# A decoder in one program: explicit orders at both ends of slot attention, other positions in both context attentions and the last feed-forward

## The reference, cut to what matters

```python
x = x + L0_attn(_layernorm(x))              # gated slot attention, 16 heads of 128, 64 slots
x = x + L0_xattn(_layernorm(x), ctx_2048)   # 256 queries on 1344 text and 257 image keys, two softmaxes
x = x + L0_ffn(_layernorm(x))               # 8 experts, top 2, and a base expert
x = x + L1_attn(_layernorm(x))              # differential attention
x = x + L1_xattn(_layernorm(x), ctx_2048)   # 256 queries on the 1601 context rows, causal at the end
x = x + L1_ffn(_layernorm(x))               # 704 inner columns, silu(g) * u
```

## Time and profile before

| | us |
|---|---|
| median of three runs | 1824.39 |
| lowest, highest run | 1814.95, 1839.33 |
| the profiled execution | 1826.9 |
| its span, first to last instruction | 1825.0 |
| mean granted TensorE clock | 0.972 |

### The profile page before, as it was taken

One profiled execution on the slowest core, in us unless ns is written; L12 is line 12 of the kernel. 1 busy time (PEld: TensorE's weight loads), 2 busy tenths in 40 slices (PEclk: granted clock), 3 DMA queues, 4 the chain that ended last, 5 costly groups with the idle time before them and its releaser, 6 DMA issues.

```text
span 1825.0 us, 51399 instructions
## 1 busy us (share of the span) xinstructions
PE 1649.1 (90%) x21686; PEld 1161.5 (64%) x21686; DVE 1279.3 (70%) x2850; ACT 855.8 (47%) x1404; POOL 558.6 (31%) x951
## 2 busy tenths in 40 slices
PE   5999999999867899899899889998988898899988
PEld 4899999998653455465466545664554455566557
DVE  6778777877577787877888353444367687888844
ACT  3343434433350465656666712442343466567652
POOL 5553544534142130501502031441021222431230
PEclk9999999999988999999999989998999999999999
DMA  3000100110008364262362383653812245554100
GB/s 127 23 25 1 47 13 13 53 43 1 20 10 172 56 132 98 47 152 51 84 119 49 70 322 111 226 185 101 160 24 40 46 82 133 87 106 77 24 2 24
DMA packets 91857, 143.94 MB, mean 79 GB/s; under 512 B 14870, under 2 KB 60123, under 8 KB 91628
## 3 DMA queue, kind: packets, MB, share of 16 engines
q1 hardware_dynamic: 87228, 127.79, 30.1%
q10 hardware_dynamic: 2528, 7.74, 1.3%
q0 software_dynamic: 1872, 5.13, 0.7%
HBM read 109.68 MB, written 32.03 MB: 78 GB/s over the span
## 4 chain that ended last, share of the span: by engine, by line
PE 67%; DVE 18%; ACT 5%; issue 5%; POOL 2%; DMA 1%; SPq 1%; DVEq 0%; ACTq 0%; POOLq 0%
PE bank L1076 17%; PE bank L1284 6%; PE bank L2029 6%; DVE shared L1357 4%; PE bank L1915 4%; PE bank L1917 3%; PE bank L1916 3%; PE bank L808 3%; PE bank L2048 3%; DVE xa_part_max L1357 3%; PE bank L2476 2%; ACT xa_e L1318 2%; PE bank L773 2%; PE bank L747 1%; PE bank L2491 1%
## 5 line engine op out<-in xcount | busy, mean ns | idle before, releaser
L1357 DVE TENSOR_REDUCE xa_part_max<-bank 128x1 f32<-128x448 f32 (+1 forms) x512 | 266.0, 567 | 22.3 <-PE bank L1076 20.3
L1318 ACT ACTIVATE xa_e<-bank 128x1024 f32<-128x1024 f32 (+1 forms) x208 | 212.2, 1024 | 124.6 <-PE bank L1076 122.5
L1318 ACT ACTIVATE ca_e<-bank 128x1024 f32<-128x1024 f32 (+2 forms) x208 | 197.4, 958 | 78.0 <-PE bank L1076 75.6
L1357 DVE TENSOR_REDUCE shared<-bank 128x1 f32<-128x400 f32 (+1 forms) x384 | 205.0, 569 | 29.2 <-PE bank L1076 25.8
L1076 PE MATMUL bank<-xa_kst,xa_qst 122*32 122x448 bf16 (+1 forms) x2048 | 182.5, 351 | 17.3 <-DVE xa_part_max L1357 9.7
L1284 PE MATMUL bank<-xa_e,xa_vaug 128*17 128x256 f32 (+1 forms) x1664 | 134.3, 381 | 6.8 <-ACT xa_e L1318 4.3
L1076 PE MATMUL bank<-xa_qst,xa_kst 128*32 128x256 bf16 (+1 forms) x3264 | 135.2, 274 | 1.3 <-DMA xa_qst<-xa_negT 1.3
L1284 PE MATMUL bank<-ca_e,ca_vaug 128*17 128x256 f32 (+2 forms) x1664 | 125.4, 373 | 3.6 <-ACT ca_e L1318 2.5
L1012 POOL TENSOR_TENSOR gsa_qk<-gsa_qk,gsa_rot 128x512 f32<-128x512 f32 x64 | 81.8, 1279 | 142.3 <-DVE gsa_rot L928 142.3
L1076 PE MATMUL bank<-xa_wkv,shared 128*32 128x256 f32 (+1 forms) x1632 | 112.6, 386 | 11.2 <-issue 4.4
L1076 PEld LDWEIGHTS bank<-xa_qst,xa_kst 128*32 128x32 bf16 (+1 forms) x3264 | 93.1, 97 | 31.8 <-issue 3.4
(11 more groups left out here) (408 smaller groups left out, 4181.0 us busy)
## 6 DMA issues: line engine op xcount, KB each, us to landing
xa_kst<-xa_k_parts SPq DMA_DIRECT2D x96, 200.1 KB, 5.0
ca_kst<-ca_k_parts SPq DMA_DIRECT2D x96, 200.1 KB, 5.2
xa_k_parts<-xa_parts SPq DMA_DIRECT2D x24, 400.2 KB, 4.7
ca_k_parts<-moe_ctx_parts SPq DMA_DIRECT2D x8, 1200.8 KB
moe_gu<-in_expert_gate_up SPq DMA_DIRECT2D x8, 1024.0 KB
shared<-in_ctxT_split ACTq DMA_DIRECT2D x4, 1601.0 KB, 8.7
moe_ctxT<-in_ctxT SPq DMA_DIRECT2D x8, 800.5 KB, 8.1
ca_cv<-in_ctx SPq DMA_DIRECT2D x4, 1536.0 KB
```

The source lines that it names most:

```text
L1318: e.activation(self.e[m % 3][0:rows, :, first:T], banks[m % 2][0:rows].rearrange("p a (h t) -> p (a h) t", t=T)[:, :, first:T], ACT.Exp, s ...
L1357: e.tensor_reduce(top, work[:, 0:hi - lo], AX.X, ALU.max).then_inc(*reduced(t, *step))
```

## The change

No instruction is added or removed; the lists are put in another order.

In slot attention `first_turns` writes out turns 0 to 3 with the norms in between, and `last_turns` turns 15 to 18 with the preparation of cross attention; turns 4 to 14 stay. In cross attention, keys, turns, queries, values and stores of the later batches get other positions, and the maxima of a unit other stretches, by its place in the batch. In context attention `pv`, `acc`, `fin`, `neg_parts`, `neg_turn`, the norms, hidden sums (`hid`), values, weights, loads and maxima move, and so do the steps of the feed-forward. The diff, cut:

```diff
+            def first_turns():
+
+                yield from (
+                    ("norm_stats", 0, 0, 2), ("norm_turn", 0, 0), ("norm", 0, 0), ("norm_turn", 0, 1), ("h_split", 0), ("w_split", 0, "q"), ("norm", 0, 1),
+                    ("w_split", 0, "k"), ("norm_stats", 0, 2, 8), ("u", 0), ("norm", 0, 2), ("qk", 0), ("norm", 0, 3), ("norm", 0, 4), ("qk", 1), ("norm_turn", 0, 2),
+                    ("norm_turn", 0, 3), ("h_split", 1), ("qk", 2), ("a", 0), ("u", 1), ("norm", 0, 5), ("norm_turn", 0, 4), ("es", 0), ("w_split", 0, "v"), ("a", 1),
+                    ("qk", 3), ("w_split", 0, "g"), ("qk", 4), ("norm_turn", 0, 5), ("ok", 0), ("h_split", 2), ("a", 2), ("norm", 0, 6), ("qk", 5), ("ok", 1), ("u", 2),
+                    ("cs", 0), ("a", 3), ("norm_turn", 0, 6), ("v", 0, 0), ("qk", 6), ("ok", 2), ("es", 1), ("a", 4), ("norm", 0, 7), ("et", 0), ("sm_max", 0),
...
+                    ("qk", 14), ("qk", 15), ("a", 12), ("v", 2, 1), ("w2", 3, 1), ("wo", 0, 0), ("wo", 0, 1), ("sm_max", 2), ("a", 13), ("o", 3))
...
-                if m == GSA_UNITS:
-                    yield "xa_w", 2
-                    for n in range(XA_TILES):
-                        yield "xk", 0, n
-                    yield "k_norm", 0
-                if m == GSA_UNITS + 1:
-                    q_steps, k_steps = list(queries(0)), list(xa_keys(0))
-                    yield from q_steps[:TB + 1]
-                    yield from k_steps[:8]
-                    yield from q_steps[TB + 1:]
-                    yield from k_steps[8:]
-                    yield "load", 0
...
-            yield from norm_steps(0, 0)
-            yield "h_split", 0
-            yield "w_split", 0, "q"
-            yield "w_split", 0, "k"
-            yield "norm_stats", 0, TB, NT
-            yield from normed_rows(1)
-            yield from normed_rows(2)
-            yield from normed_rows(3)
-            for m in range(GSA_UNITS + 3):
-                if m < GSA_UNITS - 1:
-                    main = list(turn(m))
-                else:
-                    main = list(weave(list(weave(list(scores(m)), list(ahead(m)))), list(behind(m)), lead=8))
-                if m < GSA_UNITS + 2:
-                    yield from weave(main, list(xa_early(m)))
-                else:
-                    yield main[0]
-                    yield from (("xv", 0, n) for n in range(XV_EARLY))
-                    yield from main[1:]
+
+            def last_turns():
+
+                yield from (
+                    ("qk", 60), ("sm_exp", 13), ("ok", 56), ("v", 14, 0), ("a", 58), ("scale", 12, 0), ("es", 15), ("rr", 12), ("ok", 57), ("a", 59), ("xa_w", 2),
+                    ("qk", 61), ("z", 26), ("gate", 26), ("z", 27), ("cs", 15), ("gate", 27), ("ot", 12, 0), ("sm_max", 14), ("scale", 12, 1), ("w2", 26, 0), ("ok", 58),
+                    ("w2", 26, 1), ("ok", 59), ("a", 60), ("ot", 12, 1), ("qk", 62), ("sm_exp", 14), ("wo", 12, 0), ("wo", 12, 1), ("ok", 60), ("w2", 27, 0),
+                    ("norm_stats", 1, 0, 2), ("w2", 27, 1), ("a", 61), ("o", 26), ("a", 62), ("norm", 1, 0), ("v", 14, 1), ("o", 27), ("ok", 61), ("qk", 63), ("z", 28),
...
+                    ("z", 29), ("w2", 28, 1), ("norm_turn", 1, 0), ("a", 63), ("xk", 0, 3), ("xk", 0, 4), ("xk", 0, 5), ("xk", 0, 6), ("ot", 13, 0), ("xk", 0, 7),
+                    ("norm", 1, 1), ("xk", 0, 8), ("xk", 0, 9), ("o", 28), ("ok", 63), ("wo", 13, 0), ("v", 15, 0), ("xk", 0, 10), ("sm_max", 15), ("w2", 29, 0),
+                    ("w2", 29, 1), ("norm_turn", 1, 1), ("xk", 0, 11), ("xk", 0, 12), ("gate", 29), ("q", 0), ("k_norm", 0), ("sm_exp", 15), ("o", 29), ("ot", 13, 1),
+                    ("q", 1), ("rr", 14), ("q_norm", 0), ("k_scale", 0, 0), ("k_scale", 0, 1), ("q_store", 0), ("k_scale", 0, 2), ("gate", 30), ("scale", 14, 0),
+                    ("scale", 14, 1), ("k_scale", 0, 3), ("k_scale", 0, 4), ("k_turn", 0, 0), ("k_scale", 0, 5), ("wo", 13, 1), ("k_store", 0, 1, None), ("ot", 14, 0),
+                    ("k_scale", 0, 6), ("z", 30), ("w2", 30, 0), ("k_turn", 0, 1), ("k_scale", 0, 7), ("norm_stats", 1, 2, 4), ("norm", 1, 2), ("k_turn", 0, 2),
+                    ("z", 31), ("k_scale", 0, 8), ("v", 15, 1), ("w2", 30, 1), ("k_turn", 0, 3), ("xv", 0, 0), ("norm_turn", 1, 2), ("q_turn", 0), ("k_turn", 0, 4),
+                    ("k_turn", 0, 5), ("ot", 14, 1), ("k_turn", 0, 6), ("o", 30), ("w2", 31, 0), ("k_scale", 0, 9), ("k_turn", 0, 7), ("gate", 31), ("k_scale", 0, 10),
+                    ("k_turn", 0, 8), ("norm", 1, 3), ("w2", 31, 1), ("k_scale", 0, 11), ("wo", 14, 0), ("k_turn", 0, 9), ("k_store", 0, 2, None), ("q_turn", 1),
+                    ("k_scale", 0, 12), ("wo", 14, 1), ("norm_turn", 1, 3), ("k_turn", 0, 10), ("k_turn", 0, 11), ("k_store", 0, 0, None), ("k_turn", 0, 12),
+                    ("norm_stats", 1, 4, 6), ("norm", 1, 4), ("o", 31), ("rr", 15), ("norm_turn", 1, 4), ("norm", 1, 5), ("ot", 15, 0), ("xv", 0, 1), ("scale", 15, 0),
+                    ("xv", 0, 2), ("scale", 15, 1), ("ot", 15, 1), ("xv", 0, 3), ("norm_turn", 1, 5), ("xv", 0, 4), ("xv", 0, 5), ("load", 0), ("wo", 15, 0),
+                    ("wo", 15, 1))
+
+            yield from first_turns()
+            for m in range(B, GSA_UNITS - 1):
+                yield from weave(list(turn(m)), list(xa_early(m)))
+            yield from last_turns()
...
-                        yield m + (1.5 if self.shown(k) is None else 2.3), ("pv", n, k, m)
+                        yield m + self.behind[self.shown(k) is not None], ("pv", n, k, m)
...
-                    yield m + 0.5, ("acc", n)
-                    yield m + 2.1, ("fin", n)
+                    yield m + self.ends[0], ("acc", n)
+                    yield m + self.ends[1], ("fin", n)
                     if self.masked:
-                        yield m - 3, ("fin_hidden", n)
+                        yield m - 0.5, ("fin_hidden", n)
...
-                        at = (m + 4, m + 8.7) if not self.masked else (m + 8.3, m + 9) if turns else (m + 2.5, m + 2.9)
-                        yield from spread(rows, *at)
-                        yield from spread(turns, m + 12.2, m + 13.2)
+                        at = (4, 8.7) if not self.masked else (6.8, 11.2) if turns else (1.9, 3)
+                        yield from spread(rows, m + at[0], m + at[1])
+                        yield from spread(turns, m + self.turned[0], m + self.turned[1])
...
-                yield hi + 0.4, ("neg_parts", n)
-                yield hi + 2, ("neg_turn", n)
+                yield hi + self.negs[0], ("neg_parts", n)
+                yield hi + self.negs[1], ("neg_turn", n)
...
+        XA.behind, XA.ends, XA.turned, XA.negs = (1.5, 2.3), (0.5, 2.1), (12.2, 13.2), (0.4, 2)
...
                 first = (b - 1) * UNITS * whole_unit
-                at, end = (first, 19) if b == 1 else (first - 10, 24)
-                parts += [spread(keys(b), at + 1, at + 7), spread(list(xa_keys(b))[:-3], at + 8, at + end), spread(queries(b), at, at + 7)]
-                parts += [spread(values(b), at + end, at + 36), [(at + end + 1.2 * p, ("k_store", b, p, at + end + int(1.2 * p) - 1)) for p in range(3)]]
-                parts.append(XA.load_steps(UNITS * b, at + end + 4, 2))
+                key, turn, query, value, store, apart, load = (
+                    ((-11.5, 4.5), (6.5, 15.5), (-10, -2.5), (9, 30.5), 15, 1, 22.5) if b == 1 else ((-14, -6), (-6, 0), (2, 12), (9, 29), 0, 3, 20))
+                parts += [spread(steps, first + lo, first + hi) for steps, (lo, hi) in (
+                    (keys(b), key), (list(xa_keys(b))[:-3], turn), (queries(b), query), (values(b), value))]
+                parts.append([(first + store + 0.6 + apart * p, ("k_store", b, p, first + store + apart * p - 1)) for p in range(3)])
+                parts.append(XA.load_steps(UNITS * b, first + load, 2))
+            ahead = ((1.5, 0.8), (1.75, 0.75), (1.55, 0.55), (1.5, 0.55))
             for n in range(B * UNITS):
...
-                parts.append(XA.max_steps(n, start - 1.5 * whole_unit, start - 0.55 * whole_unit))
+                parts.append(XA.max_steps(n, *(start - u * whole_unit for u in ahead[n % UNITS])))
...
+        CA.behind, CA.ends, CA.turned, CA.negs = (1.6, 2.6), (0.8, 1.4), (16.2, 18.7), (0.7, 2.5)
...
-                parts.append([((b * batch - 5 if b else unit / 3) + i, ("hid", b, i)) for i in range(TB)])
+                parts.append([((b * batch + 8.5 if b else 5.33) + i, ("hid", b, i)) for i in range(TB)])
                 if 0 < b < B - 1:
-                    parts.append([(b * batch + 10.2, ("values", b + 1, int(b * batch + 10.2) - 1)), (b * batch + 2 * unit + 1, ("values_copy", b + 1))])
+                    parts.append([(b * batch + 16.2, ("values", b + 1, int(b * batch + 16.2) - 1)), (b * batch + 28.5, ("values_copy", b + 1))])
                 if b == 1:
```

(22 more changed lines are left out.)

73 lines of the change are left out of this document (removed), and 7 rows, old and new, of tables (units, wo_in).

## The result

The changed kernel takes 1773.09 us (median of four runs, 1770.01 to 1776.11), beside four of the kernel before at 1831.58 (1814.95 to 1839.33). The ratio is 0.969 with a 95% interval of 0.961 to 0.977, so it is faster by 3.1%. Beside the second set of experiments it was measured again: 1775.13, ratio 0.966 (0.961 to 0.971). The forecast was 1785, that is 42 us less than the profiled execution's 1826.9; the profiled execution of the changed kernel has a span of 1768.0, 57 less than the 1825.0 of before.

A forecast was written before the change was run, and what follows sets the result against it. PE was taken as the bound, busy 1649 of 1825 us. Terms -5 - 17 - 8 - 7 - 5 = -42 against 1826.9 gave 1785; the forecast's own range was 1763 to 1789, 8 in 10 1763 to 1812.

The forecast's parts named there:

- all parts pay: Whole kernel: the forecast case, every stage's term pays, 42 us less, 1785 us; chance 0.50.
- The start: Start of slot attention: fewer norms and transposes ahead of the first projection, beginning 6.2 us sooner; -5, ends -8.9 and -1.5.
- The tail: Slot attention's last turns: key work and last units' softmax get cover, barrier wait goes; -17, ends -19 and -6.
- SyncE's 3.4 us at the barrier: Barrier after slot attention: PE's 3.4 us wait for SyncE's issues would be covered, stores and load lying beside work.
- near the most: Tail of slot attention: -17 taken close to the limit of -19, because DVE's 77.3 us busy leave room.
- Cross attention: Body of cross attention: a quarter of 34 idle us won by new positions; -8, ends -22 and +8.
- The weighing of the bunch: Cross attention, batches 2 and 3: key splits in 6 tiles, not 16, overload DVE, costing 6.5 us for two batches.
- Context attention: Body of context attention: a quarter of 28.5 idle us won, most staying as DVE is 84% busy; -7, ends -19 and +5.
- The last unit and the feed-forward: End of kernel: last negation's wait halves, two other waits go, slow clock partly won back; -5, ends -10 and +1.
- The waits of 1.69 and 2.12: Feed-forward: PE's waits for a norm chain and at `down` behind the newest `hidden` lose their cause, -3.8.
- some +1: Last unit: PE waits for the last `fin`'s accumulator copy and perhaps masks, as that `fin` precedes all `hidden`.
- the slower rival: Context attention: wider-spaced loads come late, each of 12 units starts 4.5 us late, +54, 1839; chance 0.05.

The follow-up runs named there:

- a_root: The changed kernel with the tail's last unit's finish and root chain put ahead of the two last norm statistics; 1772.04 us, ratio 0.964 to the kernel before.
- a_same: The changed kernel itself measured once more, nothing altered; 1775.13 us, ratio 0.966 to the kernel before.
- b_half: The kernel before, with plain maxima of units 1 to 3 of context attention taken over half of each chunk's columns; ratio 0.999.
- b_ca: The kernel before with only the new positions of context attention, without those of the feed-forward; ratio 0.988.
- a_oldflow: The changed kernel with the old offsets of both attentions' walk (pv, accumulator copy, finish, negation, norms); ratio 0.975 to the kernel before.
- a_oldwl: The changed kernel with old places of values and weights, and a load's four parts 2.5 tiles apart, not 4.5; ratio 0.969 to the kernel before.

## Why the prediction was right, and where not

The sign, the case (all parts pay) and the range were right; 1773 lies in the forecast's own 1763 to 1789. The sum of the terms was 42, and the parts gave 57 to 64. By the table four terms gave 28 us more than forecast and two gave 7 less; 64 would have been the very end of the range. So it was its width that held it, and not the terms.

**The start** (-5): the first projection begins at 14.5, earlier than the 17 to 18 forecast, and the stretch gives 6.9. The mechanism held, only the size was off: what stands ahead of the first projection takes 8.4 us less, not 6.2, and some 1.3 of it were lost again in turns 0 to 3 (91.9 from there to projection 16, not 90.6).

**The tail** (-17): -13.1. From projection 61, where the forecast's stretch began, to the barrier it is 114.1 us, not 104 to 110. SyncE's 3.4 us at the barrier went fully: PE's wait there is 0.6 us. Of the chain's waits, those for key splits fell from 4.2 to 1.4, with one of 2.3 behind the same splits new at the value matmuls, and those for scaled keys only from 4.9 to 3.8. The step that failed is "near the most", with DVE's room in the stretch as its reason. DVE's total was free, but its 26 small instructions of a norm and a root chain stood in a row, and PE waited 7.7 us behind them; `a_root` takes 6.9 of `a_same`'s 8.0 away, and the barrier comes 5.0 us sooner.

**Cross attention** (-8): -12.1. The weighing of the bunch against DVE's 2.40 us per tile was wrong in sign; the bunch pays. The forecast's mark for units 4 to 7, 120 to 123 us, fits the first trace (121.8) and proves little, since the old order gives 123.4 to 126.4 and the new one 121.8 to 125.8. It named batch 2 with them, whose units 8 to 11 took 103.2 before and not 125; there most of the gain lies.

**Context attention** (-7): -25.3 with the last negation's part. This is the term that was missed by far. It took a quarter of PE's idle 28.5 us, because DVE was busy 84%. Three things were wrong with that. DVE's work was not the bound in units 0 to 3, the ones tried (`b_half`). PE's idle time understates what a wait costs: the clock falls behind it, which by estimate makes some 7 of the 25 us, and more than half of the 10 us that busy time lost. And the weights were seen only as POOL's delay, worth one wait of 3.0. That wait did not go with the new places (2.79 in `b_ca`, 1.72 in the changed kernel's first trace), while putting large loads and POOL's work back costs 5 to 12 us by other waits; the two waits of kind "issue" at 1546 and 1553 us (5.4 us) stood in the list of PE's waits and were passed over, because nothing in the kernel releases them. The far end of the term was 19, so even its bound was too near.

**The last unit and the feed-forward** (-5): -2 for the negation and -0.7 for the rest. The last negation's wait fell from 3.16 to 1.30, as forecast, but mostly not for the reason given: one addition still takes 1.59 us beside a split on DVE, and with the splits in their old places (`b_ca`) the wait is 1.30 too. With the splits moved and the old offsets (`a_oldflow`) it is 2.52. So the moved split is worth 0.6, and the later offsets of the negation, `neg_turn` above all, the other 1.2. The waits of 1.69 and 2.12 went as forecast, and a new one of 3.41 for the last norm, behind the earlier `hidden` steps, took their place. The "some +1" for such a wait was too small.

**The stage between** (0): experts and differential attention gave 5.4 us that the forecast had not. It varies between 367 and 380 us. Most of that is in its first 60 to 70 us, in which the DMA engines are full with expert weights. PE waits there for the base expert's second layer: 2.3 to 8.0 us in the kernel before and the five built on it, 0.8 in five of the eight traces of the changed kernel and those built on that, and 4.3 to 7.3 in the other three. The changed kernel and its repetition are one of each kind (371.1 and 377.4), so the order alone doesn't decide it. Why it is mostly shorter with the new order was not tried and stays open.

**Late loads** (the slower rival): no load delayed its unit in the changed kernel. The delay it named exists, though. With the weights in their old places and the wide spacing, a query load came 6.2 us late, once.

The 3 us that hung on the rule of the Trainium skill ("SBUF — State Buffer", the section on the two separate sides) were not paid, but the rule was not put to the test: the last unit's first mask began at 1696.75, as the last of the moved splits on DVE ended (1695.54 + 1.23), and took 0.42 us. The rule itself agrees with the addition of 1.59 us beside a DVE instruction with two SBUF inputs of 1.62.

## What to carry to other kernels

Before a stage is sized by the idle time of an engine, take the list of its waits and ask of each what could cover it; a busy share of 83% on the second engine was no proof that it bounds, and a wait costs more than its length where the clock falls behind it. Look at where large loads fall: with them back next to a unit's start, PE waited 6.2 us for a query load and 4.9 us for the small DMAs of a negation here, neither of which uses what the large loads bring. A chain of small instructions on one engine should have the other engine's free-standing work beside it, and then look at what the next stage does with the time.

## What the runs showed of the hardware that was not expected

The granted clock fell to half behind PE waits of 3 us and more, and such a wait then cost more than its length. In units 4 to 7 before it is 0.51 from 1557, behind the wait of 3.75 us, and 0.50 from 1570.7, behind the wait of 3.01 that ends at 1570.62. In the changed kernel's repetition no wait in these units is longer than 1.3 us, and the clock is 1.00. It is not every such wait: one of 2.9 us in the change left it at 1.00.

The longer PE waits for which the profile shows no releaser ("issue"), 3 to 5 us, came where the DMA share of the 5 us before was about 1 (1.03 and 1.10 at 1545 to 1555 us before, 1.06 in `a_oldwl`, 0.90 in the change). The one of 3.75 us before ends at 1556.84, and POOL's wait of 3.85 for the last of the feed-forward's weights at 1556.91. The same program had one of 2.9 us in one execution of the change, and none longer than 0.8 in these units in another. The page lists 2.8 MB on a DMA queue of kind "instruction", which would fit a late instruction stream, but that is a guess: no run tried it.

A kernel's stretches differ by up to 5 us between executions of the same order (units 4 to 7 of context attention 81.6 and 76.5 in the changed kernel), while the 321.3 us of slot attention's regular turns repeat to 0.1 us. One trace against another is not enough for a step of 3 us in the attentions.
